# Group norm and layer norm ahead of a Mamba layer: batch 0 first, by halves of 512 pixels, with part of batch 1 on GpSimd

## The chip, the cores and the metric

One core of one Trainium2 chip runs the whole program. The metric is the device time of one launch in microseconds (us). All data is float32 and x is (2, 256, 32, 32): two batches (b), 256 channels in two tiles (t) of 128 partitions, 1024 pixels.

## The reference, cut to what matters

```python
x = x + _L0_conv_ref(_gn(x), ...)     # Mamba layer
x = x + _L1_conv_ref(_gn(x), ...)     # linear attention with a 5x5 depthwise conv

def _gn(v, G=32, eps=1e-05):          # groups of 8 channels, mean and variance over 8 x 1024 values
    ...
    return ((g - m) / jnp.sqrt(s + eps)).reshape(v.shape)

# start of _L0_conv_ref
x = _clamp(x)                                     # to +-10
xs = x.reshape(B, C, L).transpose(0, 2, 1)
xs = _clamp(_layernorm(xs, norm_w, norm_b))       # over the 256 channels of a pixel
xz = xs @ in_proj_w.T                             # 256 -> 2 x 512
xin, z = jnp.split(xz, 2, axis=-1)
xc = conv1d(xin, conv_w)                          # 4 taps along the pixels, causal
xc = jax.nn.silu(xc + conv_b)
xdbl = xc @ x_proj_w.T                            # dt, B and C of the scan
...
```

## The kernel before, in words

Every engine's program is written out by hand: its instructions run in the order of the code, and semaphores tie the engines together. The change is in the head, all that comes before the projections of the Mamba layer.

In the head VectorE takes the statistics of both batches (`group_sums`, L1465: bn_stats by 512, then bn_aggr); TensorE averages them over groups of 8 channels by a matmul (`group_mean`, `group_var`); ScalarE makes the reciprocal deviation (`group_rstd`, Ln and Exp). VectorE applies mean and deviation and clamps (`group_apply`, L1486: two tensor_scalar over 128x1024 for each of four tiles, in place in X). TensorE then sums each pixel over its channels with a matrix of 1/256 (`pixel_mean`, L1013: 4 matmuls of 128x512 a batch), VectorE subtracts (`pixel_center`), ScalarE squares, TensorE sums the squares (`pixel_var`), ScalarE makes the deviation (`pixel_rstd`), and VectorE multiplies by it, applies weight and bias, and clamps (`pixel_scale`, L1503: three operations over 128x1024 for each tile). Each of these steps is done for b = 0 and then for b = 1.

Then TensorE runs `project_in` (L1057; 4 matmuls of 128x512 each): x0, x1, x2, x3 for batch 0, `xdbl(0, 0)` and `(0, 1)`, x4 and x5 (batch 1), `xdbl(0, 2)` and `(0, 3)`, z0 and so on. ScalarE does `first_tap` for x0 to x2 (L662), loads the Silu table and runs `silu_conv` (L666), which frees `xdbl`. VectorE, behind the head, runs `convolve(0)` to `convolve(6)` one after the other (L1533: three scalar_tensor_tensor of L1544 each, and from convolve(3) on a tensor_scalar of L1537 ahead of them). GpSimd sets some tiles to constants, multiplies DIAGD (L523) and then waits for `correct(0)`, far behind.

Eight PSUM banks are used as four pairs. A table says who uses each pair next, and `LEFT_BY_HEAD` (L290) says when the head has left it. SP's queue loads x, the weights, and then spreads the taps of the later layer to DRAM (`spread_weights`, L349); all that is issued behind no step of the head but GpSimd's constants.

Of the kernel before, what the change touches and what calls it, by code (L numbers as in the profile page):

```python
# [10 lines left out]
P = 128  # L11
B = 2
# [39 lines left out]
def mamba_attention_kernel(nc, a, out):  # L52
    with ExitStack() as ctx:
# [133 lines left out]
        MEAN_PAIR = (3, 2)  # L187
# [66 lines left out]
        def stored(slot, upto):  # L254
# [35 lines left out]
        LEFT_BY_HEAD = (("ln_lnv", 2), ("ln_lnv", 1), ("ln_cent", B * CT), ("ln_cent", CT))  # L290
# [41 lines left out]
        def _(sp):  # L332
# [4 lines left out]
            sp.wait_ge(S["dtw_set"], 1)  # L337
# [4 lines left out]
            sp.wait_ge(S["taps_zero"], 1)  # L342
# [4 lines left out]
            sp.dma_start(patch_rows[:, P * 8 * AREA:], a["cst"][0:B * QT, 2, P - 8:]).then_inc(S["st_end"], 16)  # L347

            def spread_weights():  # L349

                sp.wait_ge(S["ld_taps"], 16 * QT)
                for t in range(QT):
                    for c in range(2):
                        for y in range(2):
                            sp.dma_start(tap_rows[c, t * P:(t + 1) * P, PATCH_W * y:PATCH_W * y + PATCH_W, :], tapped(t, HD * y + PATCH_W * c)).then_inc(S["st_taps"], 16)
                sp.wait_ge(S["ld_mix"], 16)
                for c in range(2):
                    sp.dma_start(PWR[64 * c:64 * c + 64].rearrange("p g o -> p (g o)"), mix_rows.unsqueeze(1).broadcast_to([HD, HD, QC])).then_inc(S["ld_pw"], 16)
# [116 lines left out]
            sp.wait_ge(S["st_end"], 16)  # L475
# [38 lines left out]
        def _(pool):  # L514
            pool.memset(EPSC[:, :], EPS).then_inc(S["eps_set"], 1)
            pool.memset(EPSA[:, :], EPS_ATT).then_inc(S["eps_set"], 1)
            pool.memset(DTW[:, :], 0.0).then_inc(S["dtw_set"], 1)
            pool.memset(wpr_flat[:, 0:QT * HD * HD], 0.0).then_inc(S["taps_zero"], 1)
            pool.memset(XDB[:, :, :], 1.0).then_inc(S["xd_one"], 1)
# [4 lines left out]
                               DD.unsqueeze(2).broadcast_to([P, DT_, P]), ALU.mult).then_inc(S["diagd_rd"], 1)  # L524

# [84 lines left out]
        def _(act):  # L610
# [5 lines left out]
            act.wait_ge(S["eps_set"], 2)  # L616
# [122 lines left out]
            first_tap(0)  # L739
            first_tap(1)  # L740
# [259 lines left out]
        def _(pe):  # L1000
# [12 lines left out]
            def pixel_mean(b):  # L1013
                pe.wait_ge(S["gn_out"], CT * (b + 1))
                for c in range(2):
                    for t in range(CT):
                        mm = pe.matmul(bank(MEAN_PAIR[b], c), ONES, XG[:, b, t, c * HALF:(c + 1) * HALF], start=(t == 0), stop=(t == CT - 1))
                mm.then_inc(S["ln_mu_ps"], 1)

            def pixel_var(b):  # L1020
                pe.wait_ge(S["ln_sq"], CT * (b + 1))
                for c in range(2):
                    for t in range(CT):
                        mm = pe.matmul(bank(VAR_PAIR[b], c), ONES, SQ[:, b, t, c * HALF:(c + 1) * HALF], start=(t == 0), stop=(t == CT - 1))
                mm.then_inc(S["ln_var_ps"], 1)
# [21 lines left out]
            for b in range(B):  # L1047
                group_mean(b)
            for b in range(B):
                group_var(b)  # L1050
            for b in range(B):
                pixel_mean(b)
            for b in range(B):
                pe.wait_ge(S["gn_rstd"], b + 1)
                pixel_var(b)
# [67 lines left out]
            project_in("x", 1)  # L1123
            project_in("x", 2)
# [261 lines left out]
            def qkv(k):  # L1386
# [3 lines left out]
                pe.wait_ge(S["gn_out"], 4 + CT * (b + 1))  # L1390
# [73 lines left out]
        def _(dve):  # L1464
            def group_sums(n):  # L1465
                b = n % B
                for t in range(CT):
                    for c in range(2):
                        dve.bn_stats(ST[:, CT * b + t, c, :], X[:, b, t, c * HALF:(c + 1) * HALF]).then_inc(S["gn_bn"], 1)
                    dve.wait_ge(S["gn_bn"], 4 * n + 2 * t + 2)  # L1470
                    dve.bn_aggr(MV[:, CT * b + t, :], ST[:, CT * b + t, :, :]).then_inc(S["gn_stat"], 1)
# [25 lines left out]

            def pixel_center(b):
                dve.wait_ge(S["ln_mu_ps"], b + 1)
                for t in range(CT):  # L1500
                    dve.tensor_tensor(XG[:, b, t], XG[:, b, t], pair(MEAN_PAIR[b]), ALU.subtract).then_inc(S["ln_cent"], 1)

            def pixel_scale(b):  # L1503

                dve.wait_ge(S["ln_rstd"], b + 1)
                for t in range(CT):
                    xt, i = XG[:, b, t], 2 * CT * b + 2 * t
                    dve.wait_ge(S["ln_cent"], CT * b + t + 1)
# [66 lines left out]

            convolve(0)
# [272 lines left out]
```

## Time and profile before

| | |
|---|---|
| median of 3 runs | 721.4 us (719.52 to 723.22) |
| the profiled execution | 720.2 us, span 718.4 us |
| mean granted TensorE clock | 0.987 |
| busy share of the span | PE 91%, VectorE 68%, ScalarE 56%, GpSimd 52% |
| head: start to first projection | 38.15 us |
| start to convolve(0) on VectorE | 44.80 us |

The span runs from the first to the last instruction; 1.8 us of the profiled execution lie around it. Times are microseconds from the start of the span. In the profile PE is TensorE's matmul, PEld its weight load, DVE VectorE, ACT ScalarE, POOL GpSimd, SP SyncE with its DMA queue SPq. A float32 matmul of 128x512 stands as two records (passes).

### The profile page before, as it was taken

The numbers are of one execution on the slowest core, as the hardware profiler recorded it, in microseconds if no ns is written. First come the engines' busy times: TensorE is split into PE (matmuls) and PEld (weight loads), VectorE is DVE, ScalarE is ACT, GpSimd is POOL, SyncE is SP. The second block draws the span as 40 slices with busy tenths as digits, with TensorE's granted clock in tenths as the row PEclk, the third lists the DMA queues.
The fourth block names the chain that finished last, engine by engine and source line by source line (L and its number), as shares of the span: only waits on it lengthen the run. The fifth ranks groups of instructions, "written<-read, shape, count | busy, mean of one in ns | idle before, by whom it ended". The sixth has DMA issues, their size and how long they took to land.

```text
span 718.4 us, 25562 instructions
## 1 busy us (share of the span) xinstructions
PE 652.0 (91%) x11564; PEld 453.2 (63%) x11564; DVE 486.1 (68%) x420; ACT 400.8 (56%) x790; POOL 376.6 (52%) x143
## 2 busy tenths in 40 slices
PE   1889986999998999989999999999788999999996
PEld 1334332688987898878998888944345555665642
DVE  5599658498989998898899988946751111233435
ACT  1434789898776777677877776402355434223010
POOL 1000256689988998888989888934000132323100
PEclk9999999999999999999999999999899999999999
DMA  7990163420073112413430100042078999994112
GB/s 210 76 70 5 44 161 121 124 58 18 20 179 92 62 33 54 114 48 91 121 78 26 38 8 18 5 160 52 0 169 191 234 235 233 194 167 75 30 29 117
DMA packets 81236, 67.51 MB, mean 94 GB/s; under 512 B 36232, under 2 KB 65928, under 8 KB 81128
## 3 DMA queue, kind: packets, MB, share of 16 engines
q1 hardware_dynamic: 80168, 65.46, 42.1%
q8 instruction: 91, 1.49, 0.9%
q10 hardware_dynamic: 960, 0.41, 0.2%
q14 instruction: 17, 0.14, 0.1%
HBM read 47.21 MB, written 16.57 MB: 89 GB/s over the span
## 4 chain that ended last, share of the span: by engine, by line
PE 66%; ACT 11%; POOL 11%; DVE 7%; issue 4%; DMA 1%; SPq 0%; POOLq 0%; ACTq 0%; DVEq 0%
PE PS L1180 21%; PE PS L1298 9%; PE PS L1398 6%; PE PS L1202 5%; POOL X L564 5%; PE PS L1064 5%; PE PS L1382 4%; POOL arena L564 3%; POOL WIN L564 3%; PE PS L1228 2%; PE PS L1316 2%; PE PS L1199 2%; PE PS L1278 1%; ACT arena L822 1%; DVE X L1633 1%
## 5 line engine op out<-in xcount | busy, mean ns | idle before, releaser
L564 POOL TENSOR_TENSOR X<-X,spare 128x2048 f32<-128x2048 f32 x32 | 146.6, 4584 | 20.7 <-DVE X L1633 10.7
L1180 PE MATMUL PS<-mid,arena 128*32 128x128 f32 x4096 | 138.4, 273 | 6.9 <-issue 5.6
L1180 PEld LDWEIGHTS PS<-mid,arena 128*32 128x32 f32 x4096 | 122.9, 110 | 18.2 <-issue 11.7
L1180 PE MATMUL PS<-WPR,arena 128*32 128x128 f32 x2048 | 129.6, 273 | 4.4 <-issue 2.3
L1180 PE MATMUL PS<-APROD,arena 128*32 128x128 f32 x2048 | 129.1, 273 | 3.6 <-issue 3.5
L1180 PEld LDWEIGHTS PS<-WPR,arena 128*32 128x32 f32 x2048 | 111.8, 110 | 15.7 <-issue 8.9
L1180 PEld LDWEIGHTS PS<-APROD,arena 128*32 128x32 f32 x2048 | 110.2, 110 | 3.2 <-issue 2.7
L822 ACT ACTIVATE arena<-arena,small 128x512 f32<-128x512 f32 (+1 forms) x150 | 99.5, 711 | 19.7 <-DVE X L1633 11.3
L589 POOL TENSOR_TENSOR arena<-arena,PWR 128x512 f32<-128x512 f32 x36 | 37.8, 1079 | 90.4 <-PE PS L1298 90.3
L564 POOL TENSOR_TENSOR WIN<-WIN,spare 128x2048 f32<-128x2048 f32 x16 | 73.4, 4585 | 9.1 <-DVE WIN L1633 6.9
L564 POOL TENSOR_TENSOR arena<-arena,spare 128x2048 f32<-128x2048 f32 x16 | 73.3, 4580 | 8.3 <-ACT mid L830 4.4
L1298 PE MATMUL PS<-arena 128*64 128x256 f32 x576 | 67.5, 382 | 1.1 <-issue 1.1
L1064 PE MATMUL PS<-X,WIN 128*128 128x512 f32 x128 | 60.9, 627 | 8.2 <-DVE X L1513 4.5
L1298 PEld LDWEIGHTS PS<-arena 128*64 128x64 f32 x576 | 39.0, 135 | 33.6 <-issue 9.1
L1633 DVE TENSOR_TENSOR_SCAN X<-arena,PS 128x1024 f32<-128x1024 f32 x22 | 50.1, 2283 | 12.1 <-PE PS L1180 5.9
L822 ACT ACTIVATE mid<-arena,small 128x512 f32<-128x512 f32 x74 | 49.1, 711 | 11.3 <-DVE X L1633 5.4
L1633 DVE TENSOR_TENSOR_SCAN X<-arena,mid,PS 128x1024 f32<-128x1024 f32 x21 | 48.9, 2340 | 5.8 <-PE PS L1180 4.8
L1064 PEld LDWEIGHTS PS<-X,WIN 128*128 128x128 f32 x128 | 24.7, 201 | 43.6 <-issue 35.7
L1633 DVE TENSOR_TENSOR_SCAN X<-mid,PS 128x1024 f32<-128x1024 f32 x21 | 48.6, 2313 | 4.1 <-PE PS L1180 3.4
L529 POOL TENSOR_TENSOR arena<-arena,mid 128x1024 f32<-128x1024 f32 x4 | 9.4, 2349 | 78.3 <-DVE mid L1555 78.3
L1202 PE MATMUL PS<-X,SELQ 128*32 128x256 f32 x512 | 49.0, 379 | 0.7 <-issue 0.7
L736 ACT ACTIVATE mid<-cst,mid 128x128 f32<-128x128 f32 x128 | 40.5, 389 | 9.9 <-PE PS L1180 9.9
(192 smaller groups left out, 1130.9 us busy)
## 6 DMA issues: line engine op xcount, KB each, us to landing
arena<-patch_rows SPq DMA_DIRECT2D x48, 324.0 KB, 6.4
arena<-dt_rows SPq DMA_DIRECT2D x56, 256.0 KB, 3.8
patch_rows<-arena SPq DMA_DIRECT2D x12, 648.0 KB, 7.9
X<-in_x SPq DMA_DIRECT2D x4, 1024.0 KB, 7.4
dt_rows<-arena SPq DMA_DIRECT2D x8, 512.0 KB, 2.6
spare<-c_rows SPq DMA_DIRECT2D x64, 64.0 KB, 2.2
tap_rows<-WPR SPq DMA_DIRECT2D x24, 88.0 KB, 8.2
small<-tap_rows SPq DMA_DIRECT2D x12, 176.0 KB, 8.3
```

The costliest lines, as they stand in the source:

```text
L564: pool.tensor_tensor(HB[s % 4], HB[s % 4], CROW[:, k % 2:k % 2 + 1, :].broadcast_to([P, QN, HALF]), ALU.mult).then_inc(S["g_rd"], 1)
L589: pool.tensor_tensor(WCONV[h % 2][:, :, y], TAPW[:, 8 * half:8 * half + 8, y].rearrange("p g y x -> p g (y x)").unsqueeze(2).broadcast_to( ...
L736: act.activation(DIAGB[k % 2][n][:, j, :], IDENT, ACT.Copy, scale=BT[:, b, 4 * h + j, QN * nq + n:QN * nq + n + 1]).then_inc(S["diagb_rd"], 1)
L822: act.activation(DECAY[q % 3][:, at + first:at + HALF], DTR[2 * b + h][g][:, i, first:HALF], ACT.Exp, scale=rates_at(b)[:, i, g, nq:nq + 1 ...
L1064: mm = pe.matmul(bank(pair_of(what, e), c), WIN[:, t, at:at + P], XG[:, b, t, c * HALF:(c + 1) * HALF], start=(t == 0), stop=(t == CT - 1))
L1180: mm = pe.matmul(PS[32 * n:32 * n + 32, 4 + i, j * P:(j + 1) * P], DXT[:, DT_ * b + g, 4 * h + j, 32 * i:32 * i + 32], DIAGB[k % 2][n][:, ...
L1199: pe.matmul(PS[32 * i:32 * i + 32, g, part], DIAGD[:, g, 32 * i:32 * i + 32], XC[:, DT_ * b + g, h * HALF + at:h * HALF + at + HALF // 2], ...
L1202: mm = pe.matmul(PS[32 * i:32 * i + 32, g, part], SUMQ[:, :], HB[s % 4][:, i, part], start=(nq == 0 and c == 0), stop=(nq == NQ - 1 and c ...
L1298: mm = pe.matmul(bank(1, q % 2)[64 * g:64 * g + 64, 256 * pp:256 * pp + 256], w, rows, start=(y == 0), stop=(y == ROWBLOCKS - 1))
L1382: mm = pe.matmul(project_bank(v), FOLDED[w][b][:, m * P:(m + 1) * P], QR[b][:, w, c * HALF:(c + 1) * HALF], start=(k == 0), stop=(k == 1))
L1398: mm = pe.matmul(bank(qkv_pair(k), c), WQ[:, u, t * P:(t + 1) * P], XG2[:, b, u, c * HALF:(c + 1) * HALF], start=(u == 0), stop=(u == CT - 1))
L1633: dve.tensor_tensor_scan(HB[s % 4][:, 2 * p:2 * p + 2, :].rearrange("p g l -> p (g l)"), DECAY[q % 3], pair(2 + p), start, ALU.mult, ALU.a ...
```

## The change

The head is cut in pieces of 512 pixels, called (b, c) with c the half. Batch 0 goes first on every engine. Batch 1's group norm (subtract, multiply, clamp) and its weight, bias and clamp behind the layer norm move from VectorE to GpSimd, 16 tensor_scalar of 128x512 in all. TensorE runs batch 1's pixel means ahead of x0 and its pixel variances between x1 and x2. VectorE scales batch 1 directly ahead of convolve(0). The semaphores of the constants are joined in one (`cleared`), and one DMA's semaphore (`st_end`) is joined with `ld_mix`.

```diff
-        MEAN_PAIR = (3, 2)
+        MEAN_PAIR = (3, 0)
...
-        LEFT_BY_HEAD = (("ln_lnv", 2), ("ln_lnv", 1), ("ln_cent", B * CT), ("ln_cent", CT))
+        LEFT_BY_HEAD = (("ln_lnv", 4), ("ln_lnv", 2), ("ld_cst", 16), ("ln_cent", 4))
...
 # GpSimd, behind DIAGD
+            def apply_second(c):
+
+                pool.wait_ge(S["gn_rstd"], B)
+                pool.wait_ge(S["gn_mid"], 4)
+                for t in range(CT):
+                    part = X[:, 1, t, c * HALF:(c + 1) * HALF]
+                    i = CT + t
+                    pool.tensor_scalar(part, part, GM[:, i:i + 1], GR[:, i:i + 1], ALU.subtract, ALU.mult).then_inc(S["in_prep"], 1)
+                    pool.wait_ge(S["in_prep"], 2 * c + t + 1)
+                    pool.tensor_scalar(part, part, CLAMP, -CLAMP, ALU.min, ALU.max).then_inc(S["in_outp"], 1)
+
+            def finish_second(c):
+
+                for t in range(CT):
+                    part = XG[:, 1, t, c * HALF:(c + 1) * HALF]
+                    i = 2 * c + t
+                    pool.wait_ge(S["ln_mul"], i + 1)
+                    pool.tensor_scalar(part, part, NW[:, t:t + 1], NB[:, t:t + 1], ALU.mult, ALU.add).then_inc(S["ln_aff"], 1)
+                    pool.wait_ge(S["ln_aff"], i + 1)
+                    pool.tensor_scalar(part, part, CLAMP, -CLAMP, ALU.min, ALU.max).then_inc(S["ln_outp"], 1)
+
+            apply_second(0)
+            apply_second(1)
+            finish_second(0)
+            finish_second(1)
...
 # ScalarE
-            for b in range(B):
-                group_rstd(b)
+            group_rstd(0)
+            squares(0, 0)
+            group_rstd(1)
+            squares(0, 1)
+            pixel_rstd(0, 0)
+            pixel_rstd(0, 1)
             act.wait_ge(S["ld_xp"], 32)
             act.activation(AN[:, :, :], AN[:, :, :], ACT.Exp).then_inc(S["a_exp"], 1)
-            for b in range(B):
-                squares(b)
-            for b in range(B):
-                pixel_rstd(b)
+            squares(1, 0)
+            squares(1, 1)
...
             first_tap(0)
+            pixel_rstd(1, 0)
+            pixel_rstd(1, 1)
             first_tap(1)
...
 # TensorE
+            def pixel_mean(b, c):
+                pe.wait_ge(S["in_outp" if b else "in_out"], 2 * c + 2)
+                for t in range(CT):
+                    mm = pe.matmul(bank(MEAN_PAIR[b], c), ONES, XG[:, b, t, c * HALF:(c + 1) * HALF], start=(t == 0), stop=(t == CT - 1))
                 mm.then_inc(S["ln_mu_ps"], 1)
...
+            group_mean(0)
+            group_var(0)
+            pixel_mean(0, 0)
+            group_mean(1)
+            pixel_mean(0, 1)
+            group_var(1)
+            pe.wait_ge(S["gn_rstd"], 1)
+            pixel_var(0, 0)
+            pixel_var(0, 1)
+            pe.wait_ge(S["gn_rstd"], 2)
+            pixel_mean(1, 0)
+            pixel_mean(1, 1)
...
             def project_in(what, e):
                 b, m = divmod(e, DT_)
                 pe.wait_ge(*freed(what, e))
-                pe.wait_ge(S["ln_out"], CT * (b + 1))
                 at = m * P if what == "x" else DI + m * P
                 for c in range(2):
+                    pe.wait_ge(S["ln_outp" if b else "ln_out"], 2 * c + 2)
...
             project_in("x", 0)
             project_in("x", 1)
+            pixel_var(1, 0)
+            pixel_var(1, 1)
             project_in("x", 2)
...
 # VectorE
+            dve.wait_ge(S["ld_x_b0"], 16)
+            group_sums(0, 0)
+            group_sums(0, 1)
             dve.wait_ge(S["ld_cst"], 16)
             dve.wait_ge(S["ld_cols"], 16)
...
+            group_deviation(0)
+            dve.wait_ge(S["ld_x_b1"], 16)
+            group_sums(1, 0)
+            apply_first(0)
+            apply_first(1)
+            group_sums(1, 1)
+            pixel_center(0, 0)
+            group_deviation(1)
+            pixel_center(0, 1)
+            pixel_scale(0, 0)
+            pixel_scale(0, 1)
+            pixel_center(1, 0)
+            pixel_center(1, 1)
...
+            pixel_scale(1, 0)
+            pixel_scale(1, 1)
             convolve(0)
```

`apply_first(c)` is batch 0's half of the old `group_apply`, `group_sums(b, t)` one tile of the old one; `pixel_scale(1, c)` only multiplies.

TensorE's order from the start up to the fourth projection, before (in every order fence L is a line, then the operation, the output and its inputs, the shape and how many; L1006 group mean, L1011 group variance, L1017 pixel mean, L1024 pixel variance, L1064 project_in, L1073 xdbl):

```order
L1006 MATMUL PS<-MV,cst 128x2 x2
L1011 MATMUL PS<-GV,cst 128x2 x2
L1017 MATMUL PS<-X,cst 128x512 x8
L1024 MATMUL PS<-arena,cst 128x512 x8
L1064 MATMUL PS<-X,WIN 128x512 x16
L1073 MATMUL PS<-mid,small 48x512 x4
```

TensorE's order of the same stretch with the change (L1037 and L1042 the group's mean and variance, L1047 and L1053 the pixel's, L1096 project_in, L1105 xdbl):

```order
L1037 MATMUL PS<-MV,cst 128x2
L1042 MATMUL PS<-GV,cst 128x2
L1047 MATMUL PS<-X,cst 128x512 x2
L1037 MATMUL PS<-MV,cst 128x2
L1047 MATMUL PS<-X,cst 128x512 x2
L1042 MATMUL PS<-GV,cst 128x2
L1053 MATMUL PS<-arena,cst 128x512 x4
L1047 MATMUL PS<-X,cst 128x512 x4
L1096 MATMUL PS<-X,WIN 128x512 x8
L1053 MATMUL PS<-arena,cst 128x512 x4
L1096 MATMUL PS<-X,WIN 128x512 x8
L1105 MATMUL PS<-mid,small 48x512 x4
```

Batch 1's four mean matmuls stand between batch 0's variances and x0, and its four variance matmuls now between x1 and x2; the number of matmuls is the same.

VectorE's order before, from the last clamp of the group norm to the second tile of the layer norm (L1501 center, L1509 multiply, L1511 weight and bias, L1513 clamp); the last three come four times in all, and convolve(0) follows:

```order
L1495 TENSOR_SCALAR X<-X 128x1024
L1501 TENSOR_TENSOR X<-X,PS 128x1024 x4
L1509 TENSOR_TENSOR X<-X,arena 128x1024
L1511 TENSOR_SCALAR X<-X,COLS 128x1024
L1513 TENSOR_SCALAR X<-X 128x1024
L1509 TENSOR_TENSOR X<-X,arena 128x1024
```

VectorE's order with the change, from batch 0's pixel centering to the first convolution (L1539 center, L1510 to L1516 batch 1's group deviation, L1548 multiply, L1552 weight and bias, L1555 clamp, L1591 convolve):

```order
L1539 TENSOR_TENSOR X<-X,PS 128x512 x2
L1548 TENSOR_TENSOR X<-X,arena 128x512 x2
L1552 TENSOR_SCALAR X<-X,COLS 128x512 x2
L1555 TENSOR_SCALAR X<-X 128x512 x2
L1548 TENSOR_TENSOR X<-X,arena 128x512 x2
L1552 TENSOR_SCALAR X<-X,COLS 128x512 x2
L1555 TENSOR_SCALAR X<-X 128x512 x2
L1539 TENSOR_TENSOR X<-X,PS 128x512 x4
L1576 TENSOR_SCALAR small<-small 128x64
L1548 TENSOR_TENSOR X<-X,arena 128x512 x4
L1591 SCALAR_TENSOR_TENSOR mid<-PS,COLS,mid 128x1021
```

Where four groups of multiply, weight and clamp over 128x1024 stood one after the other, two of half size are left, and batch 1's four multiplications stand right ahead of convolve(0).

## Rows read from the trace of the kernel before

**Rows 1.** Chain of waits, head and first projections: start us, us, engine, tile, line, instructions.

```profile
1.24 8.24 DMA X<-in_x
17.41 5.54 PE PS L1017 x8
...
26.55 3.69 PE PS L1024 x8
...
38.15 12.25 PE PS L1064 x24
50.42 1.20 ACT mid L662
...
63.13 1.85 PE PS L1073 x8
```

**Rows 2.** Busy time by stretch; PEclk is TensorE's granted clock (1.00 is 2.4 GHz).

```profile
17.40:21.00 3.60, 3.59 (x5) 1.53 (x6) 2.78 (x4) 0.00 (x0) 0.00 (x0) 1.00 0.47 29
21.00:26.00 5.00, 5.00 (x13) 2.14 (x11) 2.35 (x2) 1.70 (x2) 0.00 (x0) 1.00 1.30 108
38.15:41.50 3.35, 3.35 (x4) 1.47 (x5) 3.28 (x4) 0.00 (x0) 0.00 (x0) 0.50 1.43 82
```

**Rows 3.** Timeline of the head: start us, us, engine line operation out<-in xcount.

```profile
8.73 0.21 DVE L1471 BATCH_NORM_AGGREGATE MV<-ST 128x2 f32<-128x12 f32 x1
9.08 0.56 PE L1006 MATMUL PS<-MV,cst 128*128 128x2 f32 x2 [9.08 <-DVE MV L1471]
12.35 0.15 DVE L1478 COPY GM<-PS 128x2 f32<-128x2 f32 x1
13.14 0.59 PE L1011 MATMUL PS<-GV,cst 128*128 128x2 f32 x2
14.36 0.81 DVE L1491 TENSOR_SCALAR X<-X,GM,GR 128x1024 f32<-128x1024 f32 x1 [0.50 <-ACT GR L624]
30.26 1.11 ACT L633 ACTIVATE arena<-PS,EPSC 128x1024 f32<-128x1024 f32 x1 [0.42 <-PE PS L1024]
44.80 11.56 DVE L1544 SCALAR_TENSOR_TENSOR mid<-PS,COLS,mid 128x1021 f32<-128x1021 f32 x9 [1.27 <-ACT mid L662]
```

**Rows 4.** Groups of VectorE by form: busy us, mean ns of one.

```profile
L1469 DVE BATCH_NORM_STATS2 ST<-X 128x6 f32<-128x512 f32 x8 | 5.0, 672 | 6.6 <-DMA X<-in_x 6.6
L1491 DVE TENSOR_SCALAR X<-X,GM,GR 128x1024 f32<-128x1024 f32 x4 | 3.2, 808 | 0.5 <-ACT GR L624 0.5
L1665 DVE TENSOR_TENSOR mid<-mid,PS 128x512 f32<-128x512 f32 x8 | 5.1, 681 | 4.5 <-PE PS L1033 4.5
L1676 DVE TENSOR_SCALAR mid<-mid 128x512 f32<-128x512 f32 x8 | 3.0, 414 | 0.0
```

**Rows 5.** Groups of GpSimd by form.

```profile
L536 POOL TENSOR_TENSOR mid<-arena,mid 128x1024 f32<-128x1024 f32 x8 | 18.9, 2366 | 8.5 <-DVE DTMAX L1564 5.3 <-PE PS L1098 3.2
L517 POOL MEMSET DTW<- 128x512 f32 x1 | 0.5, 524 | 0.0
L577 POOL COPY arena<-small 128x192 f32<-128x192 f32 x12 | 3.8, 345 | 50.5 <-DMA small<-tap_rows 50.1
```

**Rows 6.** Timeline of the second layer's head: GpSimd beside two multiplications of VectorE, then VectorE alone.

```profile
490.47 6.64 POOL L589 TENSOR_TENSOR arena<-arena,PWR 128x512 f32<-128x512 f32 x6
564.74 3.11 POOL L589 TENSOR_TENSOR arena<-arena,PWR 128x512 f32<-128x512 f32 x3 [26.24 <-PE PS L1298]
494.57 3.10 DVE L1673 TENSOR_TENSOR mid<-mid 128x512 f32<-128x512 f32 x2 [1.93 <-ACT mid L648]
501.25 1.27 DVE L1673 TENSOR_TENSOR mid<-mid 128x512 f32<-128x512 f32 x2
```

**Rows 7.** Timeline behind the head: what starts late, and who is waited for.

```profile
56.39 1.06 ACT L666 ACTIVATE mid<-mid 128x1024 f32<-128x1024 f32 x1 [1.45 <-DVE mid L1544]
61.59 1.06 ACT L666 ACTIVATE mid<-mid 128x1024 f32<-128x1024 f32 x1 [4.14 <-DVE mid L1544]
19.70 23.30 SPq L355 DMA_DIRECT2D tap_rows<-WPR  x24
70.49 1.28 ACT L736 ACTIVATE WPR<-cst,mid 128x128 f32<-128x128 f32 x4
87.44 3.92 DVE L1544 SCALAR_TENSOR_TENSOR mid<-PS,COLS,mid 128x1021 f32<-128x1021 f32 x3
```

More of the change, by code:

```diff
@@ L345, in _ @@
             sp.dma_start(mix_rows.rearrange("i (g o) -> i g o", o=HD), a["pw"].rearrange("(g i) o -> i g o", i=HD)).then_inc(S["ld_mix"], 16)
-            sp.dma_start(patch_rows[:, P * 8 * AREA:], a["cst"][0:B * QT, 2, P - 8:]).then_inc(S["st_end"], 16)
+            sp.dma_start(patch_rows[:, P * 8 * AREA:], a["cst"][0:B * QT, 2, P - 8:]).then_inc(S["ld_mix"], 16)
             def spread_weights():
@@ L474, in _ @@
             sp.wait_ge(S["st_taps"], 16 * QT * 4)
-            sp.wait_ge(S["st_end"], 16)
             load_taps(0)
@@ L1464, in _, with group_sums @@
         def _(dve):
[L1465 to L1471, printed above, removed]
+            def group_sums(b, t):
+                for c in range(2):
+                    dve.bn_stats(ST[:, CT * b + t, c, :], X[:, b, t, c * HALF:(c + 1) * HALF]).then_inc(S["gn_bn"], 1)
+                dve.wait_ge(S["gn_bn"], 4 * b + 2 * t + 2)
+                dve.bn_aggr(MV[:, CT * b + t, :], ST[:, CT * b + t, :, :]).then_inc(S["gn_stat"], 1)
             def group_deviation(n):
@@ L1484, in group_deviation, with apply_first @@
                 dve.tensor_tensor(GV[:, cols], GV[:, cols], MV[:, cols, 1], ALU.add).then_inc(S["gn_v"], 1)
+            def apply_first(c):
+                dve.wait_ge(S["gn_rstd"], 1)
+                for t in range(CT):
+                    part = X[:, 0, t, c * HALF:(c + 1) * HALF]
+                    dve.tensor_scalar(part, part, GM[:, t:t + 1], GR[:, t:t + 1], ALU.subtract, ALU.mult).then_inc(S["in_pre"], 1)
+                for t in range(CT):
+                    part = XG[:, 0, t, c * HALF:(c + 1) * HALF]
+                    dve.wait_ge(S["in_pre"], 2 * c + t + 1)
+                    dve.tensor_scalar(part, part, CLAMP, -CLAMP, ALU.min, ALU.max).then_inc(S["in_out"], 1)
@@ L1515, in _, with pixel_center @@
-            for b in range(B):
-                dve.wait_ge(S[f"ld_x_b{b}"], 16)
-                group_sums(b)
+                    i = CT * b + t
+                    dve.tensor_scalar(XG2[:, b, t], X[:, b, t], GM[:, i:i + 1], GR[:, i:i + 1], ALU.subtract, ALU.mult).then_inc(S["gn_out"], 1)
+            def pixel_center(b, c):
+                dve.wait_ge(S["ln_mu_ps"], 2 * b + c + 1)
+                for t in range(CT):
+                    part = XG[:, b, t, c * HALF:(c + 1) * HALF]
+                    dve.tensor_tensor(part, part, bank(MEAN_PAIR[b], c), ALU.subtract).then_inc(S["ln_cent"], 1)
@@ new lines, in pixel_scale @@
+            def pixel_scale(b, c):
+                dve.wait_ge(S["ln_rstd"], 2 * b + c + 1)
+                dve.wait_ge(S["ln_cent"], 4 * b + 2 * c + 2)
+                rs = RS[:, b, c * HALF:(c + 1) * HALF]
+                parts = [XG[:, b, t, c * HALF:(c + 1) * HALF] for t in range(CT)]
+                for t in range(CT):
+                    dve.tensor_tensor(parts[t], parts[t], rs, ALU.mult).then_inc(S["ln_mul" if b else "ln_self"], 1)
+                if b == 0:
+                    for t in range(CT):
+                        dve.wait_ge(S["ln_self"], 4 * c + t + 1)
+                        dve.tensor_scalar(parts[t], parts[t], NW[:, t:t + 1], NB[:, t:t + 1], ALU.mult, ALU.add).then_inc(S["ln_self"], 1)
+                    for t in range(CT):
+                        dve.wait_ge(S["ln_self"], 4 * c + t + 3)
+                        dve.tensor_scalar(parts[t], parts[t], CLAMP, -CLAMP, ALU.min, ALU.max).then_inc(S["ln_out"], 1)
```

100 lines of the change are left out of this document (30 added, 70 removed).

## The prediction

> **What bounds the kernel now.** I read the chain of waits first, then the granted clock by stretch, then the timeline of the head, and last the groups by form for prices. The chain runs through the head step by step: x arrives at 9.5, the pixel means take 5.54, the variances 3.69, and TensorE gets its first projection at 38.15 [rows 1]. The head is one serial walk in which each engine mostly waits for another. The passes of TensorE's matmuls tell its speed: where the granted clock is 0.50 (1.2 GHz), 3.35 us hold four passes, so 0.86 us each; between 17.4 and 21.0 they are as long, though that row prints 1.00, and behind 21.0 a pass takes 0.43 [rows 2]. So both bursts that follow an idle stretch begin at half speed.
>
> Behind the head two things run. TensorE does x0 to x2 from 38.15 to 50.40 [rows 1], and VectorE's convolutions start at 44.80 and run without a gap [rows 3]. The Silu of convolve(2) starts at 56.39 and that of convolve(3) at 61.59, each when VectorE has finished the convolution [rows 7]. The start of convolve(0), which I call S, therefore decides, and it is 44.80 now.
>
> **The change, part by part.** I walk the new head with the durations of these rows.
>
> Batch 0's statistics end at 8.94. The group mean starts at 9.08 and takes 0.56; the deviation takes 0.8 (12.35 to 13.14); from the group variance to the first apply it is 1.22 (13.14 to 14.36) [rows 3]. That gives 9.64, 10.45, 11.67. VectorE is meanwhile in one tile of batch 1's sums, two bn_stats of 0.67 and an aggregate of 0.21 [rows 3, 4], about 1.5, so the apply starts at 12.0 and not at 14.36. A clamp of 128x512 is 0.41; the tensor_scalar with two column operands is 0.81 for 1024, which I take as 0.5 for 512 [rows 4]. Back to back a little of each overlaps, and a half (two of each) is 1.6. Half 0 is ready at 13.6, half 1 at 15.2, and the rest of batch 1's sums at 16.7.
>
> TensorE's pixel mean (0,0) is four passes. It comes 3.7 us earlier than 17.41, again behind an idle stretch, so I charge 0.86 a pass: 13.7 to 17.1. Batch 1's group mean (0.6) follows, then mean (0,1), 1.7 at full speed and 3.4 at half; I take the middle, 2.5, and keep both ends. That is 20.2. Group variance and ScalarE's two steps bring batch 1's deviation at 21.3, and GpSimd starts there.
>
> Batch 0 goes on: center (0,1) until 21.5 (two of 0.68 that overlap a little [rows 4]), squares until 22.6, variances until 24.3 (eight passes of 0.43). ScalarE's Ln on 128x1024 takes 1.11 [rows 3]; two steps on a half I take as 1.25. Deviation (0,0) stands at 23.8, behind the first variance. VectorE's scaling of a half is two multiplications (1.27 the pair [rows 6]), two affine (0.9) and two clamps (0.7) less overlap, 2.75. Alone it would end at 26.65 and 29.4.
>
> **GpSimd's price** is in no row, since it runs no tensor_scalar here. From below a memset of 128x512 is 0.52; from above a tensor_tensor of 1024 is 2.37, so at most 1.2 for 512; a copy of 192 columns is 0.345, which with the memset's slope gives about 0.62 for 512 [rows 5]. A tensor_scalar reads one tensor as the copy does, so I take 0.7 and keep 0.52 and 1.25. Eight of them from 21.3 end at 26.9.
>
> **Contention.** GpSimd then runs beside VectorE's scaling. In the second layer two multiplications with both inputs in SBUF took 3.10 us while GpSimd was in its six products, and 1.27 without it; GpSimd's six took 6.64, where three alone take 3.11 [rows 6]. So VectorE lost 0.9 on each and GpSimd 0.2 on each of two or so. Here four or five of GpSimd's operations (some 3 us) fall into the scaling. For GpSimd I add 0.8: 27.7, mean (1,1) until 29.4. For VectorE the loss lies between 0.8 (only the multiplications, short waits) and 4 (each of four to five operations loses 0.9); I take 2.5, about GpSimd's own busy time there. Batch 0 is then ready at 31.9.
> The Trainium skill, "SBUF — State Buffer", section "Who interferes with whom", says that a VectorE instruction with two SBUF inputs, and also one in a 2-port performance mode such as a tensor_scalar, locks GpSimd out or is locked out for a whole instruction. The trace agrees for the two inputs (3.10 against 1.27); no row has a fast tensor_scalar beside GpSimd. By that rule the loss would be near the 2.5 to 4 end, and the sum would lose up to 1.5 us of its gain.
>
> **To S.** x0's second half waits for 31.9 and ends at 33.6; x1 at 37.0; both variances of batch 1 at 40.5; deviation at 41.7; two multiplications at 43.0. GpSimd's `finish_second(0)` begins beside the last of these; I add 0.7 (0 to 1.8 by the pair above). S = 43.7, 1.1 earlier than 44.80. x0 itself is 4 us earlier, but the chain x1, variances, deviation, multiply now stands in front of convolve(0), where only first_tap stood.
>
> **Behind S.** Before, Silu(1) ended about 10.1 behind S because first_tap(2) (50.42 [rows 1]) and the table load held ScalarE; with x2 done near 44 it ends about 8.9 behind S. x5 then ends at S + 17.1, and Silu(3), bound by VectorE, at S + 17.9 (62.65 before [rows 7]); `xdbl` of tile 3 needs 1.05 more: S + 19.0, against 64.98, which is S + 20.2 [rows 1]. That is 1.2 more gain. Gain = (44.8 - S) + 1.2 = 2.3. GpSimd's finish_second ends near S + 4, and x4, which needs it, starts at about S + 10. The convolutions don't feel GpSimd: one beside a product took 3.92 as the others did [rows 7]. The taps' DMAs, which this change doesn't move, are issued by 43.0 and have landed long before the 70.49 at which ScalarE uses them [rows 7]. `st_end` under `ld_mix` and the joined constants cost nothing: what they wait for is over by then. What follows is the same program, moved by 2.3.
>
> Against the profiled execution: 720.2 - 2.3 = 717.9. It lies 1.2 below the median, so the median should go from 721.4 to 719.1.
>
> **The rivals.** *Faster by more*: GpSimd's operation costs 0.55, VectorE loses only 0.8, and mean (0,1) runs at full speed. Batch 0 is ready at 29.4, x0 ends at 31.9 to 31.1, S = 41.3 to 40.5, gain 4.7 to 5.5: 716.3. For it: the memset's 0.52 and that the products lost little. Against it: the pair at 3.10.
>
> *Slower*: GpSimd's tensor_scalar costs what its tensor_tensor does. Eight of 1.25 end at 31.4, with waits at 32.4, and VectorE does only five or six operations until then instead of twelve, so batch 0 is ready at 34.9, x0 ends at 36.6, S = 46.0 + 1.8 = 47.8, and the gain is -1.8: 723.2. It decides from about 1.0 us for an operation, where S passes 46.0.
> By "GPSIMD Engine Reference", section 3.1, of the Trainium skill, one-input bodies run at 1.03 to 1.8 cycles an element (768 ns for 512 elements), an estimate of 0.6 to 0.8 us, which speaks for my value; no run here shows it yet.
>
> *No gain*: TensorE falls back to half speed, since its head is now many short bursts with gaps at 24 to 32. x0, x1 and the variances of batch 1 are twelve matmuls, 24 passes; at 0.43 more for the first six to eight passes they give back 2.6 to 3.4: 721.6 to 722.4. Before, only the 4.5 us of idle ahead of 38.15 brought 0.50 [rows 2]; gaps of 1 us did not.
>
> **How the numbers follow.** A measurement of this kernel tells about 0.5% (3.6 us) from no change. Forecast 0.48 (719.1), faster by more 0.24 (716.3), slower 0.16 (723.2), no gain 0.12 (about 721.9). The forecast, the slower case and no gain mostly lie within 0.5%; where the slower case and half speed come together (725.8) it is beyond, some 0.06. So faster 0.24, same 0.70, slower 0.06. The range takes in the ends 716.3 and 723.2 with a scatter of 1: 715.3 to 724.2.
>
> **What would show it.** In the changed profile: GpSimd's tensor_scalar near 0.7 us; VectorE's L1548 to L1555 for batch 0 stretched while GpSimd runs; x0 from about 30, convolve(0) at 43.7; x2's first_tap no longer the last thing ahead of the Silu table; `xdbl` of tile 3 at about S + 18; the distance from there to the end as before. I am wrong if S lies outside 41 to 46, or if the distance from `xdbl` to the end changes by more than 1 us.

## The result, and the profile after

The changed kernel takes 730.35 us (median of 4 runs, 728.75 to 734.91) against 720.95 (4 runs): a ratio of 1.0146, 95% interval 1.0098 to 1.0195. A second measurement of it, beside other kernels, gave 1.0151. It is 9.4 us slower, where 719.1 and no measurable change were forecast, and it lies outside the range of 715.3 to 724.2. Medians and ratios leave out slow executions, which only mult_add_hidden below had (three of ten, 854 to 1694 us).

| | before | after |
|---|---|---|
| the profiled execution | 720.2 us, span 718.4 | 728.75 us, span 727.0 |
| mean granted clock | 0.987 | 0.980 |
| first projection starts | 38.15 us | 38.4 us |
| convolve(0) starts | 44.80 us | 52.5 us |
| fourth xdbl ends | 64.98 us | 72.7 us |
| GpSimd busy | 376.6 us | 396.6 us |

The chain of waits of the changed kernel, through the head up to the xdbl (start us, us, engine, tile, line), answers to [rows 1]. L1047 is the pixel mean, L1053 the variance, L1096 project_in, L1105 xdbl, L532 and L534 GpSimd's subtract-multiply and clamp:

```profile
17.63 2.61 PE PS L1047 x4
...
20.99 2.09 POOL X L532
23.16 0.61 POOL X L534
...
23.87 3.13 POOL X L532
27.09 0.66 POOL X L534
...
27.85 3.14 POOL X L532
31.07 0.66 POOL X L534
...
31.82 2.09 POOL X L532
33.99 0.62 POOL X L534
34.66 3.78 PE PS L1047 x4
38.44 7.50 PE PS L1096 x16
45.93 3.45 PE PS L1053 x8
...
50.78 1.77 DVE X L1548 x2
52.55 1.20 DVE mid L1591
...
60.30 3.47 PE PS L1105 x8
63.78 7.06 PE PS L1096 x16
70.84 1.85 PE PS L1105 x8
```

From 20.99 to 34.61 nothing but GpSimd's eight operations of batch 1 is on the chain: 13.6 us, where the forecast had 6.4. A subtract-multiply takes 2.09 or 3.13 us, a clamp 0.61. TensorE waits for them with batch 1's means, and x0 stands behind the means in its queue.

The second loss is TensorE's clock. Busy time by stretch of the changed kernel, with the columns of [rows 2]:

```profile
34.66:38.44 3.78, 3.78 (x5) 1.71 (x6) 0.00 (x0) 0.00 (x0) 0.00 (x0) 0.50 1.40 76
38.44:42.40 3.96, 3.96 (x9) 1.67 (x9) 1.39 (x3) 1.23 (x2) 0.00 (x0) 0.86 1.31 93
56.20:60.30 4.10, 0.03 (x1) 0.03 (x1) 4.03 (x5) 1.12 (x2) 0.75 (x2) 0.97 0.00 0
60.30:63.80 3.50, 3.50 (x9) 0.75 (x9) 3.43 (x3) 1.00 (x1) 0.00 (x0) 0.55 0.02 5
121.50:127.00 5.50, 5.43 (x10) 2.25 (x12) 3.66 (x6) 5.50 (x13) 5.50 (x3) 0.69 0.14 57
```

Three bursts behind an idle stretch run wholly or in part at half speed (1.2 GHz): mean (1,1) and the first passes of x0, behind 4.8 us without a matmul; the first xdbl, behind 4.1 us; and a projection at 121.57, behind 2.0 us. In the kernel before, x0 began at half speed too (38.15, [rows 2]), but the first xdbl came 0.3 us behind x3 and its eight passes took 1.92 us, and the same projection took 3.70 us, though it stood behind 2.4 us of idle (114.25).

### The profile page after: what moved, and what is told of

The parts are those of the page before. It is cut to its first block, busy times and chain, and to the rows that moved or that the text cites. A ratio compares the mean times of both kernels' runs of the same rounds, so it can differ in the third digit from the quotient of the medians.

```text
span 727.0 us, 25597 instructions
## 1 busy us (share of the span) xinstructions
PE 656.5 (90%) x11564; PEld 455.4 (63%) x11564; DVE 484.6 (67%) x428; ACT 402.9 (55%) x798; POOL 396.6 (55%) x159
## 4 chain that ended last, share of the span: by engine, by line
PE 69%; POOL 12%; ACT 8%; DVE 6%; issue 5%; DMA 1%; POOLq 0%; ACTq 0%; DVEq 0%
PE PS L1214 23%; PE PS L1332 9%; PE PS L1236 6%; PE PS L1432 6%; POOL X L589 5%; PE PS L1096 5%; PE PS L1416 4%; POOL WIN L589 3%; POOL arena L589 3%; PE PS L1262 2%; PE PS L1350 2%; PE PS L1233 2%; POOL X L532 1%; PE PS L1047 1%; PE PS L1312 1%
## 5 line engine op out<-in xcount | busy, mean ns | idle before, releaser
L1214 PEld LDWEIGHTS PS<-WPR,arena 128*32 128x32 f32 x2048 | 113.4, 110 | 13.8 <-issue 8.1
L1096 PE MATMUL PS<-X,WIN 128*128 128x512 f32 x128 | 60.9, 626 | 3.2 <-DVE mid L1596 2.0
L1096 PEld LDWEIGHTS PS<-X,WIN 128*128 128x128 f32 x128 | 25.0, 202 | 40.0 <-issue 32.0
L1432 PE MATMUL PS<-mid,WIN 128*128 128x512 f32 x96 | 43.1, 595 | 2.2 <-DVE mid L1533 2.2
```

The source lines that it names most:

```text
L1214: mm = pe.matmul(PS[32 * n:32 * n + 32, 4 + i, j * P:(j + 1) * P], DXT[:, DT_ * b + g, 4 * h + j, 32 * i:32 * i + 32], DIAGB[k % 2][n][:, ...
L1432: mm = pe.matmul(bank(qkv_pair(k), c), WQ[:, u, t * P:(t + 1) * P], XG2[:, b, u, c * HALF:(c + 1) * HALF], start=(u == 0), stop=(u == CT - 1))
```

## The experiments

Eleven runs follow, ten of other kernels and one of the changed kernel again. Each is compared with runs of the kernel before on the same chip, whose medians were 720.65 to 721.83. Three chips were used, so runs of different ones are compared by their ratios.

### What a GpSimd tensor_scalar costs

```diff
+            pool.wait_ge(S["a_rd"], 1)
+            src, to = X[:, 0, 0, 0:HALF], DXB[:, 1, 0:HALF]
+            for r in range(2):
+                pool.tensor_scalar(to, src, GM[:, 0:1], GR[:, 0:1], ALU.subtract, ALU.mult)   # L542
+                pool.tensor_scalar(to, src, GM[:, 0:1], GR[:, 0:1], ALU.add, ALU.mult)        # L544
+                pool.tensor_scalar(to, src, GR[:, 0:1], GM[:, 0:1], ALU.mult, ALU.add)        # L546
+                pool.tensor_scalar(to, src, GR[:, 0:1], GM[:, 0:1], ALU.mult, ALU.subtract)   # L548
+                pool.tensor_scalar(to, src, NB[:, 0:1], NW[:, 0:1], ALU.subtract, ALU.mult)   # L550
+                pool.tensor_scalar(to, src, NW[:, 0:1], NB[:, 0:1], ALU.mult, ALU.add)        # L552
+                pool.tensor_scalar(to, src, 0.5, 1.5, ALU.subtract, ALU.mult)                 # L554
+                pool.tensor_scalar(to, src, GM[:, 0:1], None, ALU.subtract)                   # L556
+                pool.tensor_scalar(to, src, CLAMP, -CLAMP, ALU.min, ALU.max)                  # L558
```

(Shortened: a semaphore stands between any two of them, and their results go nowhere.)

> The kernel before, with 18 tensor_scalar of 128x512 added on GpSimd (nine kinds, each twice), in the stretch from about 43 us where it idles and VectorE runs convolutions; their results go nowhere. Theory 1 (the operation decides: subtract as first operation is slow on GpSimd): subtract-then-multiply costs about 2.08 us with the columns of mean and deviation, with the columns of bias and weight, and with constants; subtract alone is slow too; add-multiply, multiply-add and min-max are 0.6 to 0.8. Theory 2 (the operands decide, the two columns in two tiles): every kind with mean and deviation costs 2.08, whatever the operation, and the kinds with bias and weight 0.77. The time of the kernel stays within 1% of before unless these 18 last past 81 us.

GpSimd's timeline of that kernel (start us, us, engine line, operation, out<-in):

```profile
43.36 2.08 POOL L542 TENSOR_SCALAR mid<-X,GM,GR 128x512 f32<-128x512 f32 x1 [34.66 <-DVE small L1552]
45.53 0.77 POOL L544 TENSOR_SCALAR mid<-X,GM,GR 128x512 f32<-128x512 f32 x1
46.40 0.77 POOL L546 TENSOR_SCALAR mid<-X,GR,GM 128x512 f32<-128x512 f32 x1
47.27 2.08 POOL L548 TENSOR_SCALAR mid<-X,GR,GM 128x512 f32<-128x512 f32 x1
49.45 2.08 POOL L550 TENSOR_SCALAR mid<-X,COLS 128x512 f32<-128x512 f32 x1
51.64 0.77 POOL L552 TENSOR_SCALAR mid<-X,COLS 128x512 f32<-128x512 f32 x1
52.49 1.92 POOL L554 TENSOR_SCALAR mid<-X 128x512 f32<-128x512 f32 x1
54.52 1.57 POOL L556 TENSOR_SCALAR mid<-X,GM 128x512 f32<-128x512 f32 x1
56.17 0.61 POOL L558 TENSOR_SCALAR mid<-X 128x512 f32<-128x512 f32 x1
```

The operation decides, not the operands. With a subtract, first or second, and whichever columns, it is 2.08 us; with constants 1.92; a subtract alone 1.57. Add-multiply and multiply-add are 0.77, min-max 0.61. The second pass gave the same within 0.02. The kernel took 719.66 us (one run; before 721.67): 25 us of GpSimd's work in its idle stretch, from 43 to 70 us, show no cost.

The prediction's 0.7 was right for the operations without a subtract. The Trainium skill, "GPSIMD Engine Reference", section "3.1 Elementwise — side-by-side cycle accounting", gives 1.03 cycles an element for up to two operations and 1.8 as a best case of a tight loop; at its 1.2 GHz that is an estimate of 0.44 to 0.77 us for 512 elements. The 0.61 and the 0.77 agree, the 2.08 doesn't. (The prediction's estimate from the same figures began at 0.6; they give 0.44.)

### The same kernel without the subtract

```diff
-                pool.wait_ge(S["gn_mid"], 4)
+                pool.wait_ge(S["gn_shift"], 1)
...
-                    pool.tensor_scalar(part, part, GM[:, i:i + 1], GR[:, i:i + 1], ALU.subtract, ALU.mult).then_inc(S["in_prep"], 1)
+                    pool.tensor_scalar(part, part, GR[:, i:i + 1], GS[:, t:t + 1], ALU.mult, ALU.add).then_inc(S["in_prep"], 1)
...
             pixel_center(0, 1)
+            dve.wait_ge(S["gn_rstd"], B)
+            dve.scalar_tensor_tensor(out=GS[:, :], in0=GM[:, CT:2 * CT], scalar=-1.0, in1=GR[:, CT:2 * CT], op0=ALU.mult, op1=ALU.mult).then_inc(S["gn_shift"], 1)
```

> The changed kernel, with GpSimd's subtract-then-multiply written as multiply-then-add (shift = -mean x deviation, made by one small operation on VectorE); everything else stays. Theory 1 (subtract is what is slow): the four operations take 0.77 us, up to 1.2 beside VectorE, GpSimd is done at about 27 to 28, convolve(0) starts at 43 to 44.5 and the kernel takes about 719 (717 to 721), as the prediction had it. Theory 2 (operands in two tiles are what is slow): they stay at 2.1 to 3.1 and the time stays at 730.

The median is 724.49, the ratio 1.0023 (0.9993 to 1.0053). Most of the loss is gone with one operation written another way. The clock in the head came back with it: mean (1,0) and mean (1,1) stand behind idle stretches of 1.0 and 2.9 us and take 1.96 and 1.98 us, and x0 and x1 take 7.03. Its timeline:

```profile
20.78 0.77 POOL L533 TENSOR_SCALAR X<-X,GR,GS 128x512 f32<-128x512 f32 x1 [11.95 <-DVE GS L1573]
26.43 1.59 POOL L533 TENSOR_SCALAR X<-X,GR,GS 128x512 f32<-128x512 f32 x1
28.11 0.92 POOL L535 TENSOR_SCALAR X<-X 128x512 f32<-128x512 f32 x1
30.91 7.03 PE L1097 MATMUL PS<-X,WIN 128*128 128x512 f32 x16
44.48 11.55 DVE L1594 SCALAR_TENSOR_TENSOR mid<-PS,COLS,mid 128x1021 f32<-128x1021 f32 x9
```

GpSimd ends at 29.0 and convolve(0) starts at 44.48; the prediction had 27.7 and 43.7. Beside VectorE the multiply-add too takes longer, up to 1.59. The time isn't the 717 to 721 that was expected: the step behind convolve(0) fails too, below.

### GpSimd held back until batch 0 is scaled

```diff
+            pool.wait_ge(S["ln_out"], 4)
             apply_second(0)
             apply_second(1)
```

> The changed kernel, with GpSimd's group norm of batch 1 held back until VectorE has scaled all of batch 0. Theory 'contention': the subtract-multiply of GpSimd is 2.08 us all four times (not 3.13 twice), and VectorE's scaling of a half takes 2.75 us instead of 3.7. Rival (the 3.13 is a matter of addresses or of the operation): two of four stay at 3.1. Batch 0 is ready at 29.4; GpSimd ends near 29.4 + 11.2 = 40.6, so convolve(0) starts near 57 to 59 and the kernel is 5 to 7 us slower than the changed one, about 735.

One run took 736.34 us. GpSimd and VectorE in that kernel:

```profile
22.50 1.29 DVE L1549 TENSOR_TENSOR X<-X,arena 128x512 f32<-128x512 f32 x2 [2.40 <-ACT arena L663]
23.71 1.00 DVE L1553 TENSOR_SCALAR X<-X,COLS 128x512 f32<-128x512 f32 x2
24.62 0.76 DVE L1556 TENSOR_SCALAR X<-X 128x512 f32<-128x512 f32 x2
25.29 1.29 DVE L1549 TENSOR_TENSOR X<-X,arena 128x512 f32<-128x512 f32 x2
...
31.14 2.07 POOL L532 TENSOR_SCALAR X<-X,GM,GR 128x512 f32<-128x512 f32 x1
```

and VectorE in the changed kernel, where GpSimd runs beside it:

```profile
23.60 1.31 DVE L1548 TENSOR_TENSOR X<-X,arena 128x512 f32<-128x512 f32 x2 [2.04 <-ACT arena L662]
...
24.84 1.36 DVE L1552 TENSOR_SCALAR X<-X,COLS 128x512 f32<-128x512 f32 x2
...
26.13 1.16 DVE L1555 TENSOR_SCALAR X<-X 128x512 f32<-128x512 f32 x2
...
27.21 1.69 DVE L1548 TENSOR_TENSOR X<-X,arena 128x512 f32<-128x512 f32 x2
```

Apart, all four subtract-multiplies take 2.07 to 2.08 and a half is scaled in 2.79 (22.50 to 25.29). Together two of four take 3.13, and the halves take 3.61 and 3.97. So the 3.13 is contention, and it goes both ways: GpSimd loses 2.1 us, VectorE 2.0. VectorE's tensor_scalar, which reads one tensor, suffers as well: a pair of clamps went from 0.76 to 1.16. No row of before could show that. That it can contend is what the Trainium skill says in "SBUF — State Buffer", section "Who interferes with whom". A wait for a whole instruction of 2 us, as its exclusive lock would have it, isn't seen: no pair lost more than 0.5. The expected start of convolve(0), 57 to 59, came out at 56.8.

### Batch 1's group norm on VectorE

`apply_second` is taken out of GpSimd's program as it stands, and VectorE runs it:

```diff
             pixel_center(0, 1)
+            apply_second(0)
+            apply_second(1)
             pixel_scale(0, 0)
```

> The changed kernel, with batch 1's group norm (eight operations of 128x512) back on VectorE, between center (0,1) and scale (0,0); only weight, bias and clamp of batch 1 stay on GpSimd. Theory 'GpSimd's group norm is the whole loss': VectorE's eight take 3.2 us (21.6 to 24.8), batch 0 is ready at 30.3, x0 ends near 32, convolve(0) starts at 41.5 to 43, and the kernel takes 716 to 719, faster than before. Rival 'the order costs, not the engine' (variances of batch 1 between x1 and x2, multiplications ahead of convolve(0), short bursts at half clock): convolve(0) not before 45 and the time is 721 or more.

The median is 719.74, the ratio 0.9963 (0.9938 to 0.9988): faster than before, by 0.4%, though 0.7 us above the expected 716 to 719. The order of the change is thus not what made it slow. Convolve(0) starts at 41.96 as expected, 2.8 us earlier than before, but the fourth xdbl ends only 1.7 earlier (63.3), and in this execution nothing of it is left at the end of the span (718.3, before 718.4). Busy time by stretch, in that kernel:

```profile
49.70:53.40 3.70, 3.61 (x9) 0.69 (x9) 3.63 (x3) 1.06 (x1) 0.00 (x0) 0.50 0.02 4
53.40:57.00 3.60, 3.60 (x9) 1.61 (x8) 3.53 (x4) 1.06 (x1) 0.00 (x0) 0.74 0.00 0
99.30:103.80 4.50, 4.46 (x26) 4.10 (x26) 1.92 (x2) 2.23 (x4) 1.33 (x1) 0.54 0.83 174
```

and before, in the same place of the program:

```profile
53.70:56.20 2.50, 2.18 (x10) 0.58 (x10) 2.43 (x3) 1.24 (x2) 0.00 (x0) 1.00 0.00 0
101.00:104.00 3.00, 2.97 (x26) 2.62 (x26) 1.40 (x2) 2.20 (x3) 1.31 (x1) 0.84 0.27 56
```

The first xdbl ran at full speed before, since TensorE had come to it straight from x3; now x3 is done early, TensorE idles for 4.1 us and begins at 1.2 GHz. Near 101 the 26 matmuls behind another idle stretch took 2.97 us then and 4.46 now, at a mean clock of 0.84 and 0.54. The stretch was 2.2 us long in both, so its length alone doesn't decide; why the clock fell further now stays open. Between the two places ScalarE's instructions keep their distance of 1.7 us.

### TensorE kept busy ahead of the xdbl

```diff
             pe.wait_ge(S["ld_xp"], 32)
+            pe.wait_ge(S["c1_rd"], 1)
+            for c in range(2):
+                for t in range(CT):
+                    pe.matmul(bank(3, c), WIN[:, t, 0:P], XG[:, 0, t, c * HALF:(c + 1) * HALF], start=(t == 0), stop=(t == CT - 1))
             xdbl(0, 0)
```

> apply_dve with four matmuls more on TensorE, ahead of the first xdbl, whose result is overwritten: they fill part of the idle stretch of 45.7 to 49.8 in which TensorE waits for the convolutions. Theory 'the idle stretch costs half speed behind it': the first eight passes of xdbl take 1.9 us and not 3.66, x4 and x5 7.06 and not 8.06, and the fourth xdbl ends 19.0 behind the start of convolve(0) and not 21.3; all up to about 100 us comes 2.3 earlier, and the end by 1 to 2.3 us: 717.5 to 718.7. Rival (xdbl is long for another reason, as its wait for Silu(1)): xdbl of tiles 2 and 3 still ends 21.3 behind.

The median is 717.24, the ratio 0.9934 (0.9904 to 0.9964). By the ratios four useless matmuls make apply_dve some 2 us faster, but the two intervals overlap; the trace shows the gain more surely. TensorE's timeline:

```profile
46.56 3.67 PE L1151 MATMUL PS<-X,WIN 128*128 128x512 f32 x8 [0.30 <-DVE mid L1595]
...
50.29 2.15 PE L1092 MATMUL PS<-mid,small 128*48 128x512 f32 x8
52.37 7.13 PE L1083 MATMUL PS<-X,WIN 128*128 128x512 f32 x16
...
59.44 2.03 PE L1092 MATMUL PS<-mid,small 128*48 128x512 f32 x8
```

The fourth xdbl ends at 61.47, 18.96 behind convolve(0) (42.51), where it was 21.3 in apply_dve. The rival had it stay. The first xdbl takes 2.15 us where it took 3.66, and x4 and x5 7.13 where they took 8.06. So the idle stretch was what halved the clock there.

### Batch 1's multiplications behind convolve(0)

```diff
-            pixel_scale(1, 0)
-            pixel_scale(1, 1)
             convolve(0)
+            pixel_scale(1, 0)
+            pixel_scale(1, 1)
```

Once on top of apply_dve:

> The kernel with batch 1's group norm on VectorE (apply_dve), and batch 1's four multiplications now behind convolve(0) instead of ahead of it. Theory 'what stands ahead of convolve(0) is on the path': convolve(0) starts when first_tap(0) is done, at about 34.2 (41.96 in apply_dve), the multiplications run at 38.6 to 42.0, convolve(1) starts at 42.0 instead of 45.8, and everything behind comes 3.8 us earlier: about 716. Rival 'the chain behind is bound elsewhere' (TensorE's half clock after its gaps): the first xdbl comes 3.8 earlier, but the end moves by less than 2 us: 718 or more.

715.40 (8 runs), ratio 0.9910 (0.9877 to 0.9942): the best of all, 6.4 us below the kernel before. VectorE's timeline:

```profile
33.84 3.92 DVE L1591 SCALAR_TENSOR_TENSOR mid<-PS,COLS,mid 128x1021 f32<-128x1021 f32 x3 [1.68 <-ACT mid L678]
...
39.98 1.77 DVE L1546 TENSOR_TENSOR X<-X,arena 128x512 f32<-128x512 f32 x2 [0.42 <-ACT arena L649]
41.67 7.72 DVE L1591 SCALAR_TENSOR_TENSOR mid<-PS,COLS,mid 128x1021 f32<-128x1021 f32 x6
```

Convolve(0) fills what was VectorE's wait for the deviation of batch 1, and xdbl follows x3 without the idle stretch (eight passes in 2.03).

And once on top of mult_add:

> mult_add (batch 1's group norm on GpSimd, without subtract) with batch 1's four multiplications behind convolve(0). Theory: convolve(0) starts at about 35.8, the multiplications at 41.1 to 44.6, convolve(1) at 44.6 instead of 48.3; the time is 3.7 us below mult_add's and about 2.5 us above late_scale's, since GpSimd beside VectorE still holds up the scaling of batch 0 by about 1.5 us and batch 1's means by more. Rival (contention costs nothing on the path): it equals late_scale within 1 us.

720.39, ratio 0.9976 (0.9947 to 1.0005). It stands 0.66% above late_scale, so some 4.7 us and not the 2.5 expected. The traces show 3.6 of it at convolve(1) (45.24 against 41.67), behind a scaling of batch 0 that GpSimd slows and behind later means; where the rest comes from wasn't shown.

### Nothing of the head on GpSimd

`finish_second(c)` runs on VectorE behind `pixel_scale(1, c)`; otherwise apply_dve.

> apply_dve with batch 1's weight, bias and clamp on VectorE too, so that GpSimd has none of the head; the eight operations stand between and behind the multiplications, ahead of convolve(0). If GpSimd's share in the end of batch 1 is worth what it hides: convolve(0) starts 2.5 us later than in apply_dve, at 44.5, and the time is 2.5 us above it, about 722. If its contention with the multiplications (1.77 for the second pair instead of 1.29) were all it brings, the two would be within 0.5 us.

723.13, ratio 1.0020 (0.9990 to 1.0049). Convolve(0) starts at 44.07, 2.1 later than in apply_dve. Leaving weight, bias and clamp of batch 1, which hold no subtract, to GpSimd is thus a gain: 2.1 us there, and 0.57% in the ratios.

### The slow operation kept, and the order changed

```diff
 # TensorE
-            pe.wait_ge(S["gn_rstd"], 2)
-            pixel_mean(1, 0)
-            pixel_mean(1, 1)
...
             project_in("x", 0)
             project_in("x", 1)
+            pe.wait_ge(S["gn_rstd"], 2)
+            pixel_mean(1, 0)
+            pixel_mean(1, 1)
+            project_in("x", 2)
             pixel_var(1, 0)
             pixel_var(1, 1)
-            project_in("x", 2)
...
 # VectorE
-            pixel_center(1, 0)
-            pixel_center(1, 1)
...
+            convolve(0)
+            pixel_center(1, 0)
+            pixel_center(1, 1)
+            convolve(1)
             pixel_scale(1, 0)
             pixel_scale(1, 1)
-            convolve(0)
-            convolve(1)
```

On ScalarE the squares of batch 1 go behind first_tap(1) and its deviations behind first_tap(2). mult_add_hidden is the same with the multiply-add.

> The changed kernel with GpSimd's slow subtract kept, but the order around it changed: TensorE runs x0 and x1 ahead of batch 1's means and x2 ahead of its variances, VectorE centers batch 1 behind convolve(0) and multiplies behind convolve(1), ScalarE squares behind first_tap(1). Theory 'the price counts only because x0 stands behind it in TensorE's queue': x0 starts at about 29 (38.4 in the changed kernel), convolve(0) at about 34.5, convolve(2) ends near 53 (56.4 in the kernel before), and the time is about 718 to 719, 11 us below the changed one. Rival 'GpSimd's work costs by its length and its contention with VectorE wherever it stands': it stays above 722.

> The same order with GpSimd's multiply-then-add in place of subtract-then-multiply. If the order alone hides GpSimd's group norm, the cheaper operation brings little: within 1.5 us of after_hidden (less contention with the scaling of batch 0, 0.5 to 1.5 us). If it is still on the path, 5 us less.

With the slow subtract: 718.77, ratio 0.9970 (0.9946 to 0.9995). Without it: 718.61 (seven runs), ratio 0.9964 (0.9939 to 0.9990). No difference is measured, and the traces agree to 0.1 us: convolve(0) starts at 34.41 and 34.30, the fourth xdbl ends at 62.1 and 62.0. GpSimd's operation costs nothing on the path in this order. With the subtract:

```profile
27.27 1.95 PE L1093 MATMUL PS<-X,WIN 128*128 128x512 f32 x4 [3.16 <-DVE X L1555]
...
31.65 2.07 POOL L532 TENSOR_SCALAR X<-X,GM,GR 128x512 f32<-128x512 f32 x1
...
34.41 3.92 DVE L1589 SCALAR_TENSOR_TENSOR mid<-PS,COLS,mid 128x1021 f32<-128x1021 f32 x3 [2.80 <-ACT mid L689]
```

x0 starts at 27.27, while GpSimd still works on batch 1, and convolve(0) at 34.41 (34.5 was expected). GpSimd is done at 34.4, x1 at 36.6, and the means follow x1 without a wait. What each of the moves brings by itself wasn't tested.

> The changed kernel itself once more, beside the two others on one chip: 728 to 732, 1.2 to 1.5% above the kernel before.

731.06 us, ratio 1.0151 (1.0098 to 1.0203). Beside it on one chip after_hidden is 12 us faster with the same operations on the same engines.

## Why the prediction was wrong

**GpSimd's price** is the step that failed first and cost most. "A tensor_scalar reads one tensor as the copy does, so I take 0.7 and keep 0.52 and 1.25": 1.25, from a tensor_tensor of 1024, was taken for an upper end, though no row excluded more. The clamp is 0.61 and fits; the subtract-multiply is 2.08. Eight operations with their contention took 13.6 us and not 6.4, and as they began 0.3 earlier than predicted, GpSimd ended at 34.6 instead of 27.7: +6.9. That the kinds of operation could differ was never asked, though the kernel has two kinds. The rival "slower" named the right mechanism and place, from about 1.0 us an operation, but with 1.25 for each it gave a loss of 1.8 us (723.2) where 9.4 was measured. Its meeting with half speed, which came true, had 725.8 and a chance of 0.06.

**Half speed in the head.** The prediction had "gaps of 1 us" and full speed for mean (1,1). The longer wait for GpSimd made a gap of 4.8 us: mean (1,1) took 3.78 for four passes instead of 1.7, and x0 and x1 7.5 instead of 6.9, together +2.7. (A gap of 3.6 us ahead of mean (1,0) cost little: 1.95 us for its four passes, 2.48 in the second trace.) In the forecast x0 also waited 0.8 for batch 0, which it didn't here, since batch 0 was ready at 31.3 (31.9 predicted). 6.9 + 2.7 - 0.8 = 8.8, and convolve(0) started at 52.5 where 43.7 was predicted.

**Behind convolve(0)** I claimed 1.2 more gain from an earlier table load: the fourth xdbl was to end 19.0 behind the start of convolve(0), where it was 20.2 before. busy has 18.96, so the walk was right for full speed. But the early x3 left TensorE an idle stretch of 4.1 us, and the xdbl behind it ran at half speed. In the changed kernel that xdbl took 3.47 us instead of 1.92, and the distance was 20.2: the gain of 1.2 was gone. In mult_add, apply_dve and all_dve x4 and x5 lost another 1 us (8.1 to 8.2 instead of 7.1), and the distances are 21.5, 21.3 and 21.4, a loss. Why the clock came back sooner in the changed kernel isn't known. So its fourth xdbl ended 8.8 + 1.2 = 10.0 later than forecast, which is 7.7 later than before.

**"The same program, moved"** held from there to about 100 us and not beyond. The changed kernel is 7.7 late at the xdbl, 7.4 at 104, 8.9 at 132, and 8.6 at the end: its projection at 121.57 takes 5.34 us for eight passes that took 3.70 before. It does so again in its second trace (5.33), so it isn't particular to one execution, but its cause stays open.

**What held:** the walk to 21 us (apply at 11.96, mean (0,0) at 13.63, GpSimd at 20.99, predicted 12.0, 13.7, 21.3); the contention on VectorE, 2.0 us against 2.5, a hit by luck, since the 2.5 came from GpSimd operations of 0.7 us that weren't so; finish_second early enough for x4; the DMAs without a part in it.

**What stays open:** the fastest and the slowest of ten runs of one kernel here lie 6 to 9 us apart. Only the changed kernel has two traces, 2.4 us apart (spans 727.0 and 729.4). They agree within 0.1 from 180 to 233 us; then the second loses 2.3 us up to 247. TensorE is idle there for 2.4 of the 7 us from 233 (1.4 in the first), and its clock from 240 to 247 is 0.76 (1.00 in the first). That such stretches make all of the spread wasn't tested. mult_add's median lies 5.4 above its forecast (724.5 against 719.1). In its trace 3.2 of it is there at the fourth xdbl (65.95 where 62.7 was forecast) and 4.6 near 104; the rest is within that spread.

## What to carry to other kernels

Moving work to an idle engine is costed by the very operation that moves, measured there: on GpSimd a subtract in a tensor_scalar cost 2.7 times an add, and the kernel that writes it as multiply-add got most of the loss back. What matters as much is what stands behind the moved work in the other queues: the same slow operations cost nothing once TensorE ran x0 and x1 ahead of the means that wait for them, and the steps behind the means were moved back with them. And a step brought forward may only leave a gap ahead of the next; on TensorE such a gap of 4.1 us cost the clock of the burst behind it.

## What the runs showed of the hardware

- GpSimd's tensor_scalar on 128x512 float32: 2.08 us with a subtract in either place and column operands, 1.92 with constants, 1.57 for a subtract alone, 0.77 for add-multiply and multiply-add, 0.61 for min-max.
- GpSimd and VectorE, both reading and writing SBUF at once: a subtract-multiply went from 2.08 to 3.13 on GpSimd, a pair of VectorE's clamps from 0.76 to 1.16.
- TensorE idle for 4.1 us, then a burst: 3.47 to 3.66 us for the eight passes of an xdbl, at or near 1.2 GHz; 2.15 or less where matmuls had run right before.
